# Transformer block on one core: q and k of two heads by seven half-size products, the rotation's sum on GpSimd, new orders and banks

## The reference, cut to what matters

```python
xn = _layernorm(x)                                # x is 16 x 512 x 256
q = einsum('bim,mhd->bhid', xn, wq)               # k and v likewise
q, k = rope(q), rope(k)       # even*cos - odd*sin | even*sin + odd*cos
s = einsum('bhid,bhjd->bhij', q, k) / 128
p = softmax(s - 1e30 * (i < j))
o = einsum('bhij,bhjd->bhid', p, v)
attn = einsum('bhid,hdm->bim', o, wo)
h = relu(s0 * concat([xn, -xn]) @ sign(k0)) * 2   # 512 -> 1024
h = relu(s1 * h @ sign(k1)) * 2                   # 1024 -> 1024
out = x + attn + s2 * h @ sign(k2)                # 1024 -> 256
```

## Time and profile before

| | |
|---|---|
| median of three runs | 1719.47 us |
| the profiled execution | 1720.49 us |
| its span, first to last instruction | 1718.7 us |
| mean granted TensorE clock | 0.996 |
| TensorE (matmul) busy | 1701.7 us, 99% |
| ScalarE busy | 1479.2 us, 86% |
| VectorE busy | 1450.2 us, 84% |
| GpSimd busy | 967.1 us, 56% |
| TensorE's share of the chain that ended last | 96% |

### The profile page before, as it was taken

The page is one execution under the profiler, slowest core; times in us unless marked ns, Lnnn a source line. Parts: engine busy times, 40 slices in busy tenths (PEclk is TensorE's granted clock), DMA queues, the critical chain, the costliest instruction groups (busy, mean ns, idle before and its releaser), DMA issues.

```text
span 1718.7 us, 34113 instructions
## 1 busy us (share of the span) xinstructions
PE 1701.7 (99%) x12600; PEld 1205.8 (70%) x12600; DVE 1450.2 (84%) x3503; ACT 1479.2 (86%) x3250; POOL 967.1 (56%) x767
## 2 busy tenths in 40 slices
PE   8999999999999999999999999999999999999999
PEld 5566767777677676776767677776776767667677
DVE  7998798887988889888887888879888898887975
ACT  6898898888988889888898888888888898888984
POOL 6764647556564565645556465564655656456522
PEclk8999999999999999999999999999999999999999
DMA  5232433424333333432434334333332434333333
GB/s 178 44 59 50 106 64 75 84 53 90 62 74 68 72 72 62 84 66 64 77 63 90 62 71 78 62 75 72 76 73 59 84 62 84 59 71 71 62 71 63
DMA packets 416405, 125.13 MB, mean 73 GB/s; under 512 B 396272, under 2 KB 415216, under 8 KB 416240
## 3 DMA queue, kind: packets, MB, share of 16 engines
q1 hardware_dynamic: 416240, 122.97, 36.1%
HBM read 14.94 MB, written 8.39 MB: 14 GB/s over the span
## 4 chain that ended last, share of the span: by engine, by line
PE 96%; DVE 2%; ACT 1%; DMA 1%; SPq 0%; issue 0%; DVEq 0%
PE bank L275 36%; PE bank L803 21%; PE bank L771 12%; PE bank L754 12%; PE bank L792 8%; PE bank L814 6%; DMA ph<-in_wv 1%; PE bank L782 0%; DVE bank L660 0%; ACT bank L498 0%; ACT ph L502 0%; DVE hb L624 0%; DVE rt L675 0%; DVE bank L632 0%; DVE tb L636 0%
## 5 line engine op out<-in xcount | busy, mean ns | idle before, releaser
L406 POOL TENSOR_TENSOR qk<-tb,qk 128x512 f16<-128x512 f32 x256 | 295.8, 1161 | 327.4 <-ACT qk L475 327.3
L403 POOL TENSOR_TENSOR tb<-tb,sin 128x512 f32<-128x512 f32 x256 | 325.3, 1274 | 271.5 <-ACT tb L472 269.6
L803 PE MATMUL bank<-hb,wa 128*128 128x256 f16 x3360 | 382.2, 273 | 0.0
L803 PEld LDWEIGHTS bank<-hb,wa 128*128 128x128 fp8e5 x3360 | 327.5, 98 | 38.9
L498 ACT ACTIVATE bank<-bank,nm,sc 128x512 f32<-128x512 f32 (+3 forms) x512 | 301.4, 589 | 2.9
L670 DVE SCALAR_TENSOR_TENSOR ph<-bank,rk,ph 128x256 f16<-128x256 f32 (+3 forms) x512 | 251.5, 544 | 27.6 <-ACT ph L502 26.9
L660 DVE CUSTOM_DVE_ANT_0 bank<-bank,mask 128x128 f32<-128x128 f32 (+3 forms) x512 | 237.9, 517 | 15.0 <-PE bank L754 14.7
L502 ACT ACTIVATE ph<-bank,rk 128x512 f16<-128x512 f32 (+3 forms) x512 | 230.6, 537 | 10.2 <-DVE rk L667 10.0
L754 PE MATMUL bank<-qk 128*128 128x512 f16 (+3 forms) x1536 | 230.1, 299 | 3.1 <-DVE tb L636 1.6
L471 ACT ACTIVATE tb<-bank 64x512 f32<-64x512 f32 x256 | 151.9, 593 | 89.0 <-PE bank L275 81.1
L771 PE MATMUL bank<-pt,v 128*128 128x512 f16 (+3 forms) x1536 | 227.1, 299 | 0.6 <-DVE hb L683 0.4
(11 more groups left out here) (140 smaller groups left out, 2622.0 us busy)
## 6 DMA issues: line engine op xcount, KB each, us to landing
out<-xnat SPq DMA_DIRECT2D x32, 256.0 KB, 2.1
xnat<-in_x SPq DMA_DIRECT2D x15, 512.0 KB, 3.9
pt<-ph SPq DMA_TRANSPOSE x128, 4.9
o<-in_k SPq DMA_DIRECT2D x1, 1024.0 KB, 7.9
v<-in_wq SPq DMA_DIRECT2D x1, 1024.0 KB, 9.9
v<-in_wk SPq DMA_DIRECT2D x1, 1024.0 KB, 11.6
ph<-in_wv SPq DMA_DIRECT2D x1, 1024.0 KB, 14.1
o<-in_wo SPq DMA_DIRECT2D x1, 1024.0 KB, 10.8
```

What stands on the lines that cost most here:

```text
L403: pool.tensor_tensor(tb, tb, SIN[:], ALU.mult).then_inc(s_crossed, 1)
L406: pool.tensor_tensor(QK[:, g % 2, 2 * w + 1, :], TB[:, (2 * g + w) % TRING, :], QK[:, g % 2, 2 * w, :], ALU.subtract).then_inc(s_qk_lo, 1)
L803: mm = pe.matmul(ps[:, 256 * u:256 * u + 256], WA[:, w, k, (2 * j + u) * 128:(2 * j + u) * 128 + 128], HB[:, h, s, k, :], start=first and ...
```

## The change

For batches 0 and 1 q and k are computed as before. From batch 2 on q and k of two heads (a pair) are computed together by seven products (`qk_product`). The features are split in two and the tokens in two. The parts of x are those that v already uses (XT, and the sums in XS). The parts of the weights are the two heads times the two halves of the features. One product holds three matmuls for q and three for k, each of 256 columns, both into one bank: 42 matmuls of 256 columns for a pair, where there were 24 of 512.

- A result bank then holds q and k of one head for one half of the tokens. `swap`, `straight`, `crossed`, `qk_hi` and `qk_lo` work on such a bank (128 x 512 as before, the half of the cos and sin table is used twice).
- Four banks are needed per pair, as before. VectorE copies a bank twice (`copy_q`) and adds the kept fifth product twice (`add_q5`), ScalarE keeps the fifth product (`keep_q5`).
- `straight` now writes into an SBUF tile TS, so a bank is free after `swap` and `straight`. The sum `rotate` is now on GpSimd and reads only SBUF.
- The four sums of weights are formed once, on GpSimd and ScalarE, in batches 0 and 1 (8 each of `ws_hi`, `ws_lo`, `ws_cast`, `ws_rest`, and 8 more `rotate`). The fifth form takes the place of a block of wq and wk.
- XS is now read until the last product of q and k in a batch, so `turn_t` of the next batch waits for it, and from batch 3 on `normalise` and `x_sums` work in a part of the tile H1 in place of xs.
- The programs of all five engines are written out anew without a loop, 14,900 lines, with another order and other banks. The loads at the start are in another order. The scratch space for DMA descriptors is set to 1024.

```diff
-TRING = 4
+TB_RING, TS_RING = 3, 4
+QK_BLOCKS = {0: (0, 0), 1: (1, 0), 2: (1, 1), 5: (0, 1)}
+QK_SUMS = {3: 0, 4: 1, 6: 2}
...
+        def rotate(pool, n):
+            ts = TS[:, n % TS_RING, :]
+            pool.tensor_tensor(ts, ts, TB[:, n % TB_RING, :], ALU.add).then_inc(s_rot, 1)
+        def crossed_pair(pool, n, half):
+            tb = two(TB[:, n % TB_RING, :])
+            pool.tensor_tensor(tb, tb, both(SIN, half), ALU.mult).then_inc(s_crossed, 1)
+        def qk_lo_pair(pool, g, half, n):
+            pool.tensor_tensor(qk_pair(g, LO, half), two(TS[:, n % TS_RING, :]), qk_pair(g, HI, half),
+                               ALU.subtract).then_inc(s_qk_lo, 1)
+        def keep_q5(act, ps):
+            act.activation(Q5[:], ps[:, :], ACT.Copy).then_inc(s_q5, 1)
-        def straight(dve, ps):
-            dve.tensor_tensor(ps[:, :], ps[:, :], COS[:], ALU.mult).then_inc(s_straight, 1)
-        def rotate(dve, g, w, ps):
-            tb = TB[:, (2 * g + w) % TRING, :]
-            dve.tensor_tensor(tb, ps[:, :], tb, ALU.add).then_inc(s_rot, 1)
+        def straight_pair(dve, n, half, ps):
+            dve.tensor_tensor(two(TS[:, n % TS_RING, :]), two(ps[:, :]), both(COS, half), ALU.mult).then_inc(s_straight, 1)
+        def copy_q(dve, src, dst):
+            dve.tensor_scalar(dst[:, :], src[:, :], 1.0, None, ALU.mult).then_inc(s_qcopy, 1)
+        def add_q5(dve, ps, dst):
+            dve.tensor_tensor(dst[:, :], ps[:, :], Q5[:], ALU.add).then_inc(s_qadd, 1)
...
+        def qk_product(pe, b, pair, p, ps):
+            f, buffer, t, c = V_PRODUCTS[p]
+            src = XS if buffer else XT[:, b % 2]
+            for w in range(2):
+                operands = three(lambda s: qk_weight(w, f, pair, s), lambda s: src[:, s, t:t + 2, c, :])
+                for n, (l, r) in enumerate(operands):
+                    end = w == 1 and n == 2
+                    mm = pe.matmul(ps[:, 256 * w:256 * w + 256], l, r, start=p in (1, 5) and w == n == 0, stop=end,
+                                   skip_group_check=True)
...
         def sync_program(sp):
-            load_x_first(sp)
-            load_x_rest(sp)
-            load_scales(sp)
-            load_k(sp, 0)
-            load_k(sp, 1)
-            load_w(sp, "q")
-            load_w(sp, "k")
-            load_cos(sp)
-            load_sin(sp)
-            load_k(sp, 2)
-            load_w(sp, "v")
-            load_x(sp, 1)
+         load_k(sp, 1)
+         load_cos(sp)
+         load_w(sp, "k")
+         load_x_rest(sp)
+         load_k(sp, 0)
+         load_x_first(sp)
+         load_scales(sp)
+         load_w(sp, "v")
+         load_x(sp, 1)
+         load_w(sp, "q")
+         sp.wait_ge(s_k0, 4)
+         load_w(sp, "o")
+         load_sin(sp)
+         load_k(sp, 2)
```

20601 lines of the change are left out of this document (14994 added, 5607 removed), and 16 rows, old and new, of the table ROTATION.

## The result

The changed kernel takes **1742.57 us** (median of 4 runs, 1737.29 to 1743.36), the kernel before in the same comparison 1718.82 (4 runs, 1717.71 to 1719.49). The ratio is 1.0132 with a 95% interval of 1.0111 to 1.0153. It is slower by 24 us where 26 us less was forecast. The profiled execution has a span of 1740.6 us beside the 1718.7 of the earlier trace rows.

What follows compares the result with a forecast made beforehand. TensorE was taken to bound the kernel: -34.4 us from smaller q and k products and +8.0 at the start give -26.4, so 1693 us from the median 1719.5, range 1683 to 1706.

Steps and rivals of the forecast that it cites:

- What bounds the kernel, and what a matmul costs: TensorE bounds the steady stretch; 512 columns cost 216.7 ns, 256 cost 109.2, so q and k products save 34.4 us.
- The start: Loads before the first q or k: half of x lands at 13.3 us instead of 3.6, costing +8 us.
- Weight sums: Batches 0 and 1: 24 instructions and 8 more sums on GpSimd, about 41 us, fit barely; cost 0.
- VectorE (0): Each batch: sums replaced by copies and additions, +0.2 us, 88% busy, 13 us spare; cost 0, covered by TensorE.
- ScalarE (0): Each batch: `keep_q5` adds 2.5 us, 92% busy instead of 88%, 8 us spare; cost 0.
- Rival 3: Each batch: ScalarE or the GpSimd chain hands over late by 0.4 to 1.2 us, total 1704 us; chance 0.18.
- Rival 2: At the normalisation GpSimd becomes the bound and scores wait for the LO part; 1735 us at 3 us a batch; chance 0.05.
- GpSimd (0): Each batch: GpSimd gains 20.4 us of sums, 78% busy instead of 57%; cost 0 while the queue keeps up.
- The end: Layer 2 and most of the last projection cover the last transposes as before: 0, with 1 us either way.

Runs made afterwards that it cites:

- the two small kernels: Kernels with only GpSimd additions and VectorE scaled subtractions, the computation left out; with both operands in SBUF, 512 columns took 1.73 us beside one or six additions.
- every edit together: Changed kernel with old load order, two GpSimd waits, weight sums for 8 of 128 columns, single-copy swaps, LO parts for 32 columns from batch 3: 1706.13 us.
- The two reliefs: Changed kernel with each swap as one copy without exchange (1729.78 us), or LO parts of probabilities and attention output for 32 columns from batch 3 (1733.64); both: 1729.31.

## Why the prediction was wrong, point by point

**What bounds the kernel, and what a matmul costs.** Right. 256 columns are 109 ns apart in the q and k products too, and 33.5 us of TensorE's own time are gone (34.4 forecast). The difference is rounding: 216.7 ns was read from six matmuls, and an unbroken row of 512 columns has 215.5, with which the sum is 33.3.

**The start (+8, ends +2.7 and +12).** The landing was right, 12.9 us where 13.3 was worked out. The effect was 12.3 us of lost time, at the upper end, but it isn't the late x alone. In the kernel before, the new loads cost 9 to 12 us. In the changed kernel they cost 10.9 us with VectorE's line blocked and 4.3 with it free. There about 5 us of the delay were made up between the statistics and the first q, as the forecast allowed. What it didn't have is the blocked line: a wait of 4.24 us and 2.9 us of slow clock behind it, 7.2 together. That +8 comes near is in part luck.

**Weight sums (0, from -2 to +3).** This is the first step that failed, the term of 0 for the weight sums: 16.4 us more were lost from 60 to 300 us. "It fits barely" was said of GpSimd's busy time, and by busy time it did fit (92 and 90 of 100). What I left out is that an unbroken row on GpSimd is no private matter. VectorE's instructions with two SBUF operands stand behind it, and the split of wo took 6.39 us. The Trainium skill (SBUF — State Buffer, "Who interferes with whom") has this rule: a VectorE instruction with two SBUF inputs contends with a GpSimd instruction that reads SBUF, and whichever comes second stands still until the first is done. By this rule the split had to wait for one GpSimd instruction, as it did in the two small kernels (1.73 us); in the changed kernel it waited for the one under way and for three and four more that began meanwhile, so there the rule alone is too mild. The forecast didn't weigh it, though it speaks directly against moving work to GpSimd. The price of this event is about 5 us from 110 to 200, and at the start up to 7, which the late x also explains. Of the 16.4 us, 7.0 stay with every edit together, and their cause is open.

**VectorE (0) and ScalarE (0), "covered by TensorE".** The second step that failed, and the largest, is "Cost 0" for both, the cover by TensorE: 21.4 us from 300 to 1600, and 5.3 behind. The busy shares were well forecast (VectorE 85% where 88% was worked out, ScalarE 90% for 92%, GpSimd 78%). The failure is in reading cover from a share. I took the spare time of 8 and 13 us a batch as a cushion. But the work doesn't come evenly. Behind each row of scores ScalarE is full for 16 us and VectorE then for 10, and TensorE's banks come free at the end of both. The two reliefs took away 7.8 and 6.9 us, 12.6 together. That is the part which the runs show to pass through these queues; 8.8 us of the 21.4 stay, and whether the added load or the new order made the waits is open.

**Rival 3 (small waits in each batch, 0.18)** was the right one, with its size off. It had 0.4 to 1.2 us a batch; it was 23.5 / 12.5 = 1.9 (104.14 us a batch are 12.5 batches in 1300 us), before 0.2. "At 88% TensorE has not one wait" was the argument against it. That sentence was true and proved nothing for 90% and other orders, since it doesn't say by how much the results were in time.

**Rival 2 (GpSimd at the normalisation, 0.05), the only slower case,** didn't happen: cutting the rotation short left the steady waits as they were (22.6 against 23.5). The kernel got slower by another way, one that I had as "still faster". I had each of the mishaps as a case by itself, and no case for three of them at once: start 12, early batches 16, steady 21 and the end 5, each of a kind that I had named or had a page for, add up to 55 us against a gain of 34.

**GpSimd (0).** Right for the steady stretch, wrong for the early batches, as above. **The end (0, 1 either way):** 5.3 us, from 5.6 down to 3.3 by the same two reliefs.

## What to carry to other kernels

That TensorE has no idle time says that every other engine's result was in time, and not by how much. A change that lengthens or reorders the fullest of the other queues must be priced by the bursts between two hand-overs, not by its busy share. Before work is moved to GpSimd, look which VectorE instructions with both operands in SBUF run beside it; two waits on GpSimd that let them pass gave 11.6 us here. And a late first load has no fixed price: 8.5 us later at the statistics were 9 to 12 us at the end in the kernel before, and in the changed kernel 4 or 11, by whether another wait stood behind it.

## What was unexpected of the hardware

- VectorE's scaled subtraction of 512 columns took 7.45 us, ten times its own 0.74, beside an unbroken row of GpSimd instructions; in a kernel of its own never more than 1.73 beside additions of the same width, and 3.12 at most in any form tried. The exclusion works both ways: beside 512 columns of VectorE's GpSimd's six additions took 7.81 us against 7.36, beside 1024 columns 8.34.
- With one operand in a bank there is no exclusion at all: 0.75 us, and 7.36 us for GpSimd's six, as the Trainium skill (SBUF — State Buffer, "Who interferes with whom") has it.
- A wait of TensorE of 4 to 5 us costs more than itself. The clock granted behind it was 0.50, which cost 2.9 us more behind the wait of 4.24 and 1.6 behind that of 4.61. Behind the wait of 1.71 us (old load order) it stayed at 1.00.
